# Routing stage of a two-layer graph and expert network: stacked group rows, degree sums on GpSimd, top-two search inside the turns

## The reference, cut to what matters

```python
# layer 0, graph part: 5 groups of nodes (25, 9, 7, 6, 6) per graph, a two-step graph convolution in each
fused[:, idx, :] += softmax(fusion_w)[g] * out_g        # only nodes 0 to 24 ever get anything
# x1 = x + fused, xln = layernorm(x1)
# layer 0, experts: routing
gate_scores = xln @ Wg.T + bg                           # 8 experts
topk_scores, topk_idx = top_k(gate_scores, 2)           # two largest, the lower index first on a tie
topk_probs = softmax(topk_scores)                       # then relu-MLPs of the two chosen experts
# layer 1, graph part
deg = (adj + I).sum(-1); dis = (deg + 1e-8) ** -0.5     # needs a sum over every row of every adj
# layer 1, experts: a shared MLP and 2 of 4 small ones
```

## Time and profile before

| what | value |
|---|---|
| median of 3 runs | 1537.96 us |
| profiled execution, its own time | 1536.0 us |
| its span in the trace | 1534.2 us |
| PE busy over the span | 1303.0 us (85%) |
| DVE busy | 1153.8 us (75%) |
| ACT busy | 916.0 us (60%) |
| POOL busy | 797.0 us (52%) |
| mean granted TensorE clock | 0.89 |

### The profile page before, as it was taken

One profiled execution on the slowest core, in us unless ns is written; L12 is line 12 of the kernel. 1 busy time (PEld: TensorE's weight loads), 2 busy tenths in 40 slices (PEclk: granted clock), 3 DMA queues, 4 the chain that ended last, 5 costly groups with the idle time before them and its releaser, 6 DMA issues. The chain is left out here.

```text
span 1534.2 us, 26804 instructions
## 1 busy us (share of the span) xinstructions
PE 1303.0 (85%) x6416; PEld 910.6 (59%) x6416; DVE 1153.8 (75%) x3916; ACT 916.0 (60%) x1747; POOL 797.0 (52%) x750
## 2 busy tenths in 40 slices
PE   5888499962556999999999999159999999999998
PEld 4666266651444777777777777136565565655665
DVE  5787465559985999999999998347767777677763
ACT  1333244430005999999999998146667666676674
POOL 3543111123006777777777774566666666666620
PEclk9999655555777999999999999669999999999999
DMA  4554444440002223323222237212122221222210
GB/s 161 185 186 149 117 122 130 125 161 0 1 1 85 80 75 80 79 74 79 80 77 75 80 78 64 62 49 69 57 76 58 68 68 56 76 59 68 69 35 22
DMA packets 136461, 124.07 MB, mean 81 GB/s; under 512 B 14164, under 2 KB 115949, under 8 KB 135278
## 3 DMA queue, kind: packets, MB, share of 16 engines
q1 hardware_dynamic: 119021, 88.03, 18.9%
q0 software_dynamic: 17408, 35.69, 10.0%
HBM read 83.89 MB, written 39.77 MB: 81 GB/s over the span
## 5 line engine op out<-in xcount | busy, mean ns | idle before, releaser
L946 POOL DMA_INDIRECT exg<-xln_scratch,eidx x288 | 324.9, 1128 | 127.4 <-issue 69.1
L1249 POOL DMA_INDIRECT yg<-expert_rows_scratch,idx x256 | 247.2, 966 | 101.4 <-issue 77.8
L1100 DVE TENSOR_TENSOR ehl<-ehr,ehh 128x512 fp32r<-128x512 f32 x288 | 197.6, 686 | 28.5 <-ACT ehh L971 28.2
L968 ACT ACTIVATE ehr<-p_eh,bc 128x512 f32<-128x512 f32 x288 | 198.4, 689 | 26.3 <-PE p_eh L1010 18.6
L971 ACT ACTIVATE ehh<-ehr 128x512 fp32r<-128x512 f32 x288 | 182.1, 632 | 9.2
L1487 DVE SCALAR_TENSOR_TENSOR xtok<-yg,prob,xtok 128x128 f32 (+1 forms) x256 | 80.1, 348 | 124.5 <-DMA yg<-expert_rows_scratch,idx 116.6
L1256 POOL TENSOR_TENSOR root_l<-pre_l,mhalf 128x4 f32<-128x4 f32 x64 | 80.7, 1262 | 130.4 <-DVE pre_l L1507 130.4
L1008 PE MATMUL p_ey<-ehh,wh 128*128 128x512 f32 x288 | 126.8, 440 | 0.8 <-DVE ehl L1100 0.8
L1008 PE MATMUL p_eh<-exh,wh 128*128 128x512 f32 x288 | 125.7, 437 | 1.5 <-DVE exl L1095 1.5
L1348 PE MATMUL p_lh<-x4t,w 128*128 128x512 f32 x256 | 122.2, 601 | 0.0
L962 ACT ACTIVATE exh<-p_ex 128x512 fp32r<-128x512 f32 x72 | 41.9, 582 | 123.5 <-PE p_ex L1004 121.6
(11 more groups left out here) (207 smaller groups left out, 3089.8 us busy)
## 6 DMA issues: line engine op xcount, KB each, us to landing
expert_rows_scratch<-eyo SPq DMA_DIRECT2D x72, 256.0 KB
xtok<-in_x_tok SPq DMA_DIRECT2D x8, 1024.0 KB, 7.1
an<-in_a_t SPq DMA_DIRECT2D x16, 512.0 KB, 4.6
xln_scratch<-xl SPq DMA_DIRECT2D x16, 512.0 KB, 3.6
at<-in_a_t SPq DMA_DIRECT2D x32, 256.0 KB, 2.8
out<-outx SPq DMA_DIRECT2D x32, 256.0 KB, 2.5
wj<-in_w_grp SPq DMA_DIRECT2D x16, 321.0 KB, 4.2
exg<-xln_scratch,eidx POOLq DMA_INDIRECT x288
```

The lines of the kernel that those rows point to most:

```text
L946: pool.indirect_dma_start(out=xg[p][:, k, :], out_offset=None, in_=xln_d, in_offset=bass.IndirectOffsetOnAxis(ap=idx[p][:, k:k + 1], axis=0))\
L968: nc.scalar.activation(hr[c % 2][:, :], p_h[c][:, :], ACT.Relu, bias=bc[p][:, c:c + 1])\
L1100: nc.vector.tensor_tensor(hl[:, c, :], hr[c % 2][:, :], hh[:, c, :].bitcast(F32), ALU.subtract)\
L1249: pool.indirect_dma_start(out=yg[p][:, c, k, :], out_offset=None, in_=y_d, in_offset=bass.IndirectOffsetOnAxis(ap=idx[p][:, c, k:k + 1], a ...
```

## The change

Four things change in the routing stage and at the start of the sorting stage.

1. `sel` and `ct` are laid out so that the group rows of an even and an odd graph stand under each other on partitions (106 rows x 4 pairs of graphs). One product of 512 columns replaces two. Its result has the nodes of even graphs on partitions 0 to 24 and those of odd graphs on 32 to 56 of PSUM; DVE adds them to `xtok` in two instructions of 25 partitions.
2. The adjacency rows are no longer reduced by DVE in each turn. POOL adds each batch's 128x1024 elements to a running sum `dsum`, right behind `root`. SP's load of adjacency rows waits for this addition, and one DVE reduction of `dsum` stands in the sorting stage.
3. The logits of a batch leave PSUM right behind the addition to `xtok` (they were last in DVE's turn), and the search for the two largest runs in the turn on 64 elements per partition, between and behind the instructions of the statistics.
4. The search on whole tiles is gone from the sorting stage, with two semaphores.

```diff
-    sel = np.zeros((GR, P), np.float32)
+    sel = np.zeros((2 * GR, 2 * 32), np.float32)
     for g, nodes in enumerate(GROUPS):
-        for n, node in enumerate(nodes):
-            sel[GOFF[g] + n, node] = 1
+        for h in range(2):
+            for n, node in enumerate(nodes):
+                sel[2 * GOFF[g] + h * GN[g] + n, 32 * h + node] = 1
...
-        lg = alloc(lgp, "lg", [P, B, E0])
-        part = alloc(lgp, "deg_parts", [P, B // (2 * R), N])
+        mask = [alloc(lgp, f"mask{k}", [P, B, E0]) for k in range(2)]
+        mb = alloc(lgp, "mb", [P, B, E0], F16)
+        dif = alloc(lgp, "dif", [P, B])
+        dsum = alloc(lgp, "deg_sums", [P, 2 * R, N])
...
-            ct = [alloc(ctx, f"ct{p}", [GR, RG, D]) for p in range(2)]
-            sel = alloc(ctx, "sel", [GR, P])
+            ct = [alloc(ctx, f"ct{p}", [2 * GR, R, D]) for p in range(2)]
+            sel = alloc(ctx, "sel", [2 * GR, 2 * 32])
+            lt = alloc(ctx, "lt", [P, RG, E0])
+            wd = alloc(ctx, "wd", [P, RG, E0])
+            tv = [alloc(ctx, f"tv{k}", [P, RG]) for k in range(3)]
...
-            p_sel = [bank(ctx, f"p_sel{p}", [P, RG, D]) for p in range(2)]
+            p_sel = [bank(ctx, f"p_sel{p}", [2 * 32, R, D]) for p in range(2)]
...
-                            src = c_d[g][0:B * GN[g], :].rearrange("(b n) d -> n b d", n=GN[g])
-                            sp.dma_start(ct[p][GOFF[g]:GOFF[g] + GN[g], :, :], src[:, bass.ds(RG * j, RG), :])\
-                              .then_inc(loaded[p], 16)
+                            src = c_d[g][0:B * GN[g], :].rearrange("(b h n) d -> (h n) b d", h=2, n=GN[g])
+                            sp.dma_start(ct[p][2 * GOFF[g]:2 * GOFF[g] + 2 * GN[g], :, :],
+                                         src[:, bass.ds(R * j, R), :]).then_inc(loaded[p], 16)
...
-                            sp.wait_ge(deg_ready, i + p + 1)
+                            sp.wait_ge(deg_ready, i + p + 2)
                             load_rows(i + p + 2, p)
                             store(i + p, p)
...
+                    def degrees(i, p):
+                        pool.wait_ge(an_loaded[p], 8 * i + 16)
+                        pool.wait_ge(deg_ready, i + p + 1)
+                        nc.gpsimd.tensor_tensor(dsum[:, :, :], dsum[:, :, :], an[p][:, :, :], ALU.add)\
+                          .then_inc(deg_ready, 1)
+
+                    nc.gpsimd.memset(dsum[:, :, :], 0.0).then_inc(deg_ready, 1)
                     roots(0, 0)
+                    degrees(0, 0)
                     roots(1, 1)
+                    degrees(0, 1)
                     with pool.Fori(2, NB - 1, 2) as i:
                         for p in range(2):
                             pool.wait_ge(xl_ready, 2 * (i + p) - 2)
                             roots(i + p, p)
+                            degrees(i, p)
...
-                            for h in range(2):
-                                last = nc.tensor.matmul(
-                                    p_sel[p][:, h * R:(h + 1) * R, :].rearrange("p r d -> p (r d)"), sel[:, :],
-                                    ct[p][:, h * R:(h + 1) * R, :].rearrange("p r d -> p (r d)"),
-                                    start=True, stop=True)
-                            last.then_inc(sel_done, 1)
+                            nc.tensor.matmul(p_sel[p][:, :, :].rearrange("p r d -> p (r d)"), sel[:, :],
+                                             ct[p][:, :, :].rearrange("p r d -> p (r d)"),
+                                             start=True, stop=True).then_inc(sel_done, 1)
...
+                    pri = cf[:, CF_PRI:CF_PRI + E0].unsqueeze(1).to_broadcast([P, RG, E0])
+
+                    def largest(dst, src):
+                        return nc.vector.tensor_reduce(dst[:, :], src[:, :, :], AX.X, ALU.max)
+
+                    def same(dst, src, v):
+                        return nc.vector.tensor_tensor(dst, src[:, :, :],
+                                                       v[:, :].unsqueeze(2).to_broadcast([P, RG, E0]), ALU.is_equal)
 
...
+                        c = j - 3
+
+                        def after(n):
+                            dve.wait_ge(tk, TK * c + n)
+
+                        def step(ins):
+                            ins.then_inc(tk, 1)
+
+                        def stats(ks):
+                            for k in ks:
+                                last = nc.vector.bn_stats(st[:, k, :], xtok[:, bass.ds(RG * b + k, 1), :])
+                            return last
+
+                        def averages(ks):
+                            for k in ks:
+                                last = nc.vector.bn_aggr(mv[q][:, k, :], st[:, k, :])
+                            return last
+
                         if second:
-                            rows = xtok[:, bass.ds(RG * b, RG), :]
                             dve.wait_ge(sel_done, j)
-                            nc.vector.tensor_tensor(rows, rows, p_sel[q][:, :, :], ALU.add).then_inc(x1_ready, 1)
+                            dve.sem_inc(passed, 1)
+                            for h in range(2):
+                                rows = xtok[0:NG, :, :].rearrange("p (b h) d -> p b h d", h=2)[
+                                    :, bass.ds(R * b, R), h, :]
+                                last = nc.vector.tensor_tensor(rows, rows, p_sel[q][32 * h:32 * h + NG, :, :], ALU.add)
+                            last.then_inc(x1_ready, 1)
+                        if last_:
+                            dve.wait_ge(lg_done, j - 2)
+                            nc.vector.tensor_tensor(lt[:, :, :],
+                                                    p_lg[:, 0:RG * E0].rearrange("p (b e) -> p b e", e=E0),
+                                                    bgs[:, :].unsqueeze(1).to_broadcast([P, RG, E0]), ALU.add)\
+                              .then_inc(lg_ready, 1)
+                        if second:
                             dve.wait_ge(x1_ready, j)
                             dve.sem_inc(passed, 1)
-                            for k in range(RG):
-                                last = nc.vector.bn_stats(st[:, k, :], xtok[:, bass.ds(RG * b + k, 1), :])
-                            last.then_inc(stat_s, 1)
+                            stats(range(2))
+                        if last_:
+                            dve.wait_ge(lg_ready, j - 1)
+                            step(largest(tv[0], lt))
+                        if second:
+                            stats(range(2, 5))
+                        if last_:
+                            after(1)
+                            step(same(wd[:, :, :], lt, tv[0]))
+                        if second:
+                            stats(range(5, RG)).then_inc(stat_s, 1)
+                        if last_:
+                            after(2)
+                            step(nc.vector.tensor_tensor(wd[:, :, :], wd[:, :, :], pri, ALU.mult))
+                        if second:
                             dve.wait_ge(stat_s, j)
                             dve.sem_inc(passed, 1)
-                            for k in range(RG):
-                                last = nc.vector.bn_aggr(mv[q][:, k, :], st[:, k, :])
-                            last.then_inc(mv_s, 1)
+                            averages(range(R))
+                        if last_:
+                            after(3)
+                            step(largest(tv[2], wd))
+                        if second:
+                            averages(range(R, RG)).then_inc(mv_s, 1)
+                        if last_:
+                            m0 = mask[0][:, bass.ds(RG * c, RG), :]
+                            m1 = mask[1][:, bass.ds(RG * c, RG), :]
+                            after(4)
+                            dve.sem_inc(passed, 1)
+                            step(same(m0, wd, tv[2]))
+                        if second:
                             dve.wait_ge(mv_s, j)
                             nc.vector.tensor_scalar(pre[q][:, :], mv[q][:, :, 1], 1e-5, None, ALU.add)\
                               .then_inc(pre_ready, 1)
-                        if first:
-                            dve.wait_ge(an_loaded[p], 8 * i + 16)
+                        if last_:
+                            after(5)
                             dve.sem_inc(passed, 1)
-                            nc.vector.tensor_reduce(part[:, bass.ds(j, 1), :].rearrange("p a n -> p (a n)"),
-                                                    an[p][:, :, :].rearrange("p m n -> p n m"), AX.X, ALU.add)\
-                              .then_inc(deg_ready, 1)
-                        if last_:
-                            dve.wait_ge(lg_done, j - 2)
-                            nc.vector.tensor_tensor(lg[:, bass.ds(RG * (j - 3), RG), :],
-                                                    p_lg[:, 0:RG * E0].rearrange("p (b e) -> p b e", e=E0),
```

(68 more changed lines are left out.)

4 lines of the change are left out of this document (removed).

## The result

| | before | after |
|---|---|---|
| median, us | 1537.55 (1534.69 to 1541.4, 20 runs) | 1540.65 (1537.87 to 1544.56, 20 runs) |
| ratio to before, 95% interval | | 1.0019 [1.0012, 1.0026] |
| profiled execution, own time / span | 1536.0 / 1534.2 | 1542.5 / 1540.6 |
| two turns of the routing loop | 19.67 | 21.70 |
| last product to the stage's last DVE instruction | 25.75 | 34.34 |

What follows compares the result with a forecast made beforehand. Two interleaved chains, each closing in two turns through product, logits, `gnb`, `xl`, store and `ct`, bound routing, with PE nearly full. Routing +24.5 and sorting -16.9 gave +7.6: execution 1536.0 to 1543.6, median 1545.5 us, range 1525 to 1557.

Steps and rivals of the forecast that it cites:

- Order on DVE and block, +5.0 and +2.2 per chain: Routing loop, `lt` to `gnb`: statistics and search between them add 5.0 us; POOL's addition blocking `gnb` adds 2.2.
- Rival B: POOL's addition does not block `gnb`: eight blocks of 2.2 us fall away, -17.6, so 1528; chance 0.19.
- The bounds of 4.9 and 6.2: Limits on the +5.0 us: search free, or none of 13 instructions overlapping and each paying 0.1 more.
- Product −1.89: Routing loop, per chain: four PE records in 3.77 us become two, saving 1.89.
- ACT −1.67: Routing loop, per chain: transposes are copied before the late `gnb`, so `xl` follows by 0.27 us, not 1.94.
- `ct`, −0.7 per chain, between 0 and −1.2: Routing loop, store to landed `ct`: same bytes over twice the partitions save 0.7 us, partly hidden by issuing five DMAs.
- First turns, +1: Routing turns 0 to 4: no reduction and its wait first, two blocks of 2.2 come in; +1 us, between -3 and +4.
- Behind the last product, +8.8: End of the routing stage: the stretch behind the last product grows from 25.75 to 34.5 us.
- Stage, +24.5: Whole routing stage: five chains +14.7 us, first turns +1, behind the last product +8.8.
- Sorting, −16.9: Start of sorting: search gone before the first count, -18.8 us; reducing `dsum` costs 1.9.
- Rival C: Search costs its upper bound, its last two steps blocked with `gnb`: 1.2 us more at eight passes, +10, 1555; chance 0.08.
- Rival D: Search and statistics hide beside PE; each chain loses 1.89, 1.67 and 0.7 us, with the 16.9 giving 1500; chance 0.03.

Runs made afterwards that it cites:

- Part 1 alone: The kernel before with only the stacked group rows (one product, two additions of 25 partitions, `ct` over twice the partitions): 1514.77 us, ratio 0.9857.
- the moved load alone: The kernel before, with SP issuing its adjacency load only once `gnb` of the turn is there, ahead of the store: 1535.42 us, ratio 0.9989.
- three small edits of order: The changed kernel with logits taken last and searched next turn, POOL's addition behind `gnb`, and next adjacency rows issued right behind `ct`: 1498.64 us, ratio 0.9737.

## Why the prediction was right and wrong

The direction was right, and the turns are longer by the named mechanism. The size was not: +7.6 in the sum, +3.1 in the medians. The terms that failed are that of `ct` and that of the first turns. That the time lies inside the range and on the forecast side is in part luck: by the edits as measured the two kernels are about even, and most of the 3.1 comes from a place that the sum did not have.

- **Order on DVE and block, +5.0 and +2.2 per chain.** Together 7.2, measured 7.03 (`lt` to `gnb` 7.43 for 0.40). The parts were split wrongly. `root` ends 5.1 behind `lt`, a little ahead of the 5.3 worked out, but the search does not: its last step `mb` starts only 5.4 behind, and `gnb` 0.5 behind that. Unblocked this is 5.89, so +5.5. The block is 1.54 in this chain and not 2.2: `mb` has 0.23 of its own, the addition has run for 0.30 when it starts, and the 0.30 that `gnb` waits behind an unblocked `mb` is gone behind a blocked one. The block hits the instruction that comes next with two operands from SBUF, `mb` in the loop and `gnb` in turns 1 and 2. So the rule quoted from the Trainium skill ("SBUF — State Buffer", "Who interferes with whom") held for the SCALAR_TENSOR_TENSOR too: 2.30 beside an addition of 2.34. The rule speaks of any GpSimd instruction that reads SBUF, and beside GpSimd's powers it did not hold: the two-operand steps of the search that start within `root` (216.15 to 217.87) take 0.22 to 0.23 as elsewhere. In the sorting stage `wide` made from `mask` and `posf` takes 1.90 beside the power of 20.91 us in the changed kernel (at 359.16), and 1.90 in the kernel before, where the power is over (at 359.37). Rival B falls. The bounds of 4.9 and 6.2 do not follow from their conditions: by an estimate from the same rows these give about +4.2 (the whole search free) and +7.0 (all 13 steps at 0.36, none overlapped).
- **Product −1.89, ACT −1.67.** −1.81 and −1.56.
- **`ct`, −0.7 per chain, between 0 and −1.2.** This step failed: −1.64, outside its bounds. Part 1 alone shows the whole of it, and the moved load alone 0.3. I had priced the layout by bytes at the rate of a window full of other transfers, 256 GB/s, and let the issue of five DMAs hide half. (The window at 107 GB/s was not of `ct` alone either: the adjacency rows are issued at 235.22, within it.) The gain is larger than even that rate allows; why is open. The rule of the Trainium skill on the number of engines ("DMA: Bandwidth & Descriptors", "Why a DMA increments its semaphore by 16 and not by 1") pointed past −0.7, toward −1.2. No run shows the number of engines by itself. Five chains by 0.94 is 4.7 of the difference: the period is 21.7 and not 22.6.
- **First turns, +1.** This term failed too: −2.1. From the first product to that of turn 5 it is 40.7, for 41.0 before, and the first one comes 1.8 earlier. The kernel before itself had its first product at 168.3 and 167.9, so 0.4 of that is spread. I had counted the gain of the product and of `ct` in none of these turns. Part 1 alone shows it: there the product of turn 5 comes at 203.30, for 209.36 before and 207.24 in the changed kernel. So the stacked rows give some 6 up to there, and the other three parts take 3.9 back.
- **Behind the last product, +8.8.** +8.6.
- **Stage, +24.5.** +16.6, of which 10.1 in five chains in place of 14.7, −2.1 in place of +1, and 8.6 in place of 8.8.
- **Sorting, −16.9.** −16.8. The first count comes 1.00 behind, and the loop behind it (L906, before L845) starts at 368.50 where it did at 368.71. Another −2.0 from there up to `ids` can't be put down to an edit: from the first count to `ids` the kernel before took 107.6 in one profile and 105.7 in the second, the changed one 107.8 with 1.9 of it for the added reduction. So by its edits the changed kernel is about even when the experts begin, and not +7.6.
- **Not in the sum: the first gather, +2.5.** Twelve instructions that do nothing here give 1.6 of it, and twelve more, on another chip, go with a short gap: it hangs on the program of GpSimd and not on the work of the edit. With the other terms at their measured sizes it is most of the 3.1 by which the medians differ.
- **Also not in the sum: layer 1, open.** It is 5.3 longer in the two profiles. Windows from its first gather to the end and 60 us behind that gather, first before, then after (length, busy times, clock, DMA share, GB/s):

```profile
969.00:1534.20 565.20, 496.23 (x2626) 310.38 (x2626) 383.78 (x2024) 353.79 (x800) 327.92 (x320) 0.95 0.21 60
1029.00:1039.00 10.00, 8.59 (x45) 4.74 (x44) 4.63 (x26) 6.98 (x17) 7.69 (x9) 1.00 0.25 74
```

```profile
970.10:1540.60 570.50, 498.04 (x2626) 312.32 (x2626) 385.35 (x2024) 354.91 (x800) 327.40 (x320) 0.95 0.22 59
1030.10:1040.10 10.00, 7.70 (x39) 4.89 (x36) 4.50 (x27) 5.57 (x11) 7.68 (x9) 0.83 0.20 47
1060.10:1070.10 10.00, 7.39 (x28) 4.07 (x28) 7.46 (x43) 5.81 (x14) 6.65 (x7) 0.83 0.12 33
```

Both stages begin at a granted clock of 0.50 (1.2 GHz) for some 55 us and then go up to 1.00 (2.4 GHz), but the changed kernel has two later windows at 0.83. Over windows of 10 us of the whole stage, what the clock is short of 1.00 adds up to 28.3 us before and 30.9 after. That is 2.6 of the 5.3, as a sum and not as a trial, and another run speaks against it: the kernel before with twelve memsets takes 570.1 there, 4.9 more than without them, though its clock is short by only 29.0. Nor does the count of instructions settle it. The four profiles of 570.1 to 571.1 all have 85 of GpSimd, but three others with 85 have 566.7 to 568.6, and three with 73 have 565.2 to 567.9. In the medians twelve memsets cost 2.0, of which the gather's gap is 1.6, so most of these 4.9 is not in them.

Rival C (search 0.1 dearer per step) came true in small. Most steps follow each other by 0.26, but the last two, `mask` and `mb`, start 0.44 and 0.46 behind the one ahead (217.24, 217.68, 218.14). At 0.26 each `mb` would have started at 217.76, ahead of the addition at 217.84; as it is, it comes behind `root` and is blocked in the place of `gnb`, as C has it. C's 10 us do not show: the chain is no longer than the main forecast has it. Rival D falls as a forecast of the whole (1500), but the stacked rows do give what it says: alone 22.5 us, where the order of DVE is left as it was. Rival B's count of eight passes leaves out one of the two blocks that the prediction puts into turns 0 to 4.

## What to carry to other kernels

A search moved into a loop is free only behind what the loop's chain needs: ask where in the turn the wait stands, and what then follows it on its engine. Run each part of a change alone: here one is worth 22.5 us by itself, the others ate it, and three small edits of order made the same parts 40 us faster than the kernel before. Where a chain waits for a DMA of few rows, try a layout over more partitions early: here it gave 1.64 us in each chain. And where two kernels differ by 0.2%, a dozen idle instructions away from the edit can move as much time as the edit (2.0 us here).

## What the runs showed of the hardware

- A f32 addition of 128x1024 on GpSimd takes 2.34 us (all 16: 2.331 to 2.346), and a DVE instruction with two operands from SBUF that starts beside it lasts to its end (2.13 and 2.30, alone 0.23 and 0.15). GpSimd's powers do not hold such an instruction: one of 1.90 takes 1.90 beside a power of 20.91 us and without it, and one of 64 elements 0.22 to 0.23 beside a power of 1.72 us.
- 217 KB in five DMAs of 512 B pieces, issued behind a store of 512 KB: the product that waits for them starts 6.64 us behind the store's issue over 53 partitions, and 5.00 over 106.
- SP's issue of these five takes 2.7 us, and up to 3.67 where a load of 512 KB and a store were issued within the 1.5 us ahead of it.
- Twelve instructions of GpSimd under idle time, 100 us ahead, made a later gap 1.6 us longer (2.77 for 1.15), with a packet on the instruction queue in it. With 24 more than the kernel before, on another chip, the gap was 1.15 again, without a packet.
- On one chip layer 1 of the same kernel took 737.5 us at a mean clock of 0.85, on another 565.2 at 0.95.
